# Weaving two instruction streams, a top-k search and four layers, on every engine of one core

## What is computed

```python
xn = _layernorm(x); s = _Ln_attn_ref(xn, ...); g = _silu(_Ln_ffn_ref(xn, ...)); x = x + s * g
```

```python
scores = jnp.einsum('bhnd,bhmd->bhnm', q, k) / jnp.sqrt(D); aw = softmax(scores)
kth = jax.lax.top_k(aw, topk)[0][..., -1:]
aws = aw * (aw >= kth); aws = aws / (aws.sum(-1, keepdims=True) + 1e-08); o_s = aws @ v
o = a * o_s + (1.0 - a) * o_l          # o_l: linear attention over softmax(q), softmax(k)
```

## Time and profile before

| | |
|---|---|
| median of 3 runs | 5734.3 us (5724.26 to 5734.64) |
| the profiled execution, its own time | 5721.85 us |
| its span | 5720.0 us |
| DVE busy, share of the span | 4273.7 us, 75% |
| PE busy | 4228.7 us, 74% |
| ACT busy | 2946.7 us, 52% |
| POOL busy | 2505.1 us, 44% |
| PE's granted clock, mean | 0.896 of full speed |

### The profile page before, as it was taken

The page is one execution under the profiler, slowest core; times in us unless marked ns, Lnnn a source line. Parts: engine busy times, 40 slices in busy tenths (PEclk is TensorE's granted clock), DMA queues, the critical chain, the costliest instruction groups (busy, mean ns, idle before and its releaser), DMA issues. The chain is left out here.

```text
span 5720.0 us, 61822 instructions
## 1 busy us (share of the span) xinstructions
PE 4228.7 (74%) x17108; PEld 2321.5 (41%) x17108; DVE 4273.7 (75%) x8380; ACT 2946.7 (52%) x5759; POOL 2505.1 (44%) x2236
## 2 busy tenths in 40 slices
PE   5876778767787677776777777786777867777676
PEld 2434434334343443434434344342443424434344
DVE  3478964799647995479953899548994489944899
ACT  3544645446454564545645456454554545545455
POOL 0245622446224562245622466214662156621565
PEclk9998989988899898988989978999889998889988
DMA  2000000000000000000000000000000000000000
GB/s 101 1 0 3 1 3 1 0 3 1 3 1 0 3 1 3 1 2 1 1 3 1 2 1 1 3 1 2 1 1 3 1 2 1 1 3 1 2 1 3
DMA packets 3553, 23.17 MB, mean 4 GB/s; under 512 B 336, under 2 KB 336, under 8 KB 2640
## 3 DMA queue, kind: packets, MB, share of 16 engines
q1 hardware_dynamic: 3152, 18.59, 0.8%
HBM read 16.23 MB, written 2.36 MB: 3 GB/s over the span
## 5 line engine op out<-in xcount | busy, mean ns | idle before, releaser
L1662 POOL TENSOR_SCALAR l_pp<-l_sc,l_m 128x512 f32<-128x512 f32 x496 | 781.8, 1576 | 642.6 <-DVE l_m L1612 618.7
L1612 DVE MAX8 l_m<-l_wk 128x8 f32<-128x512 f32 x1536 | 979.9, 679 | 0.0
L1356 PE MATMUL bank<-consts,l_pp 128*128 128x128 f32 x2048 | 396.7, 326 | 499.5 <-POOL l_pp L1669 490.0
L227 PE MATMUL bank<-l_v,l_pt 128*128 128x99 f32 x4096 | 645.6, 311 | 147.4 <-ACT l_pt L1402 131.4
L1432 ACT ACTIVATE l_sc<-bank 128x512 f32<-128x512 f32 x512 | 303.0, 594 | 743.3 <-PE bank L227 742.4
L1608 DVE MATCH_REPLACE8 l_wk<-l_m,l_wk 128x512 f32<-128x512 f32 x1024 | 683.6, 675 | 0.0
L227 PEld LDWEIGHTS bank<-l_v,l_pt 128*128 128x128 f32 x4096 | 610.1, 228 | 177.7 <-ACT l_pt L1402 173.3
L227 PE MATMUL bank<-l_km,hold 128*128 128x512 f32 x1024 | 649.2, 724 | 42.5 <-DVE l_ol L1579 18.1
L1356 PEld LDWEIGHTS bank<-consts,l_pp 128*128 128x128 f32 x2048 | 280.6, 166 | 936.7 <-POOL l_pp L1669 803.8
L1669 POOL TENSOR_TENSOR l_pp<-l_pp,l_ex 128x512 f32<-128x512 f32 x496 | 630.3, 1271 | 26.7 <-ACT l_ex L1439 4.9
L1220 POOL TENSOR_TENSOR l_hc<-l_h,l_cn 128x1024 f32<-128x1024 f32 x128 | 302.4, 2362 | 674.1 <-DVE l_h L1170 674.1
(11 more groups left out here) (359 smaller groups left out, 8347.7 us busy)
## 6 DMA issues: line engine op xcount, KB each, us to landing
weights<-weights_dram SPq DMA_DIRECT2D x1, 11014.0 KB, 28.9
hold<-x_dram SPq DMA_DIRECT2D x9, 256.0 KB, 2.6
out_dram<-x SPq DMA_DIRECT2D x9, 256.0 KB, 3.6
consts<-consts_dram SPq DMA_DIRECT2D x1, 1503.0 KB, 32.0
rotary<-consts_dram SPq DMA_DIRECT2D x1, 1024.0 KB, 34.0
```

The source lines that it names most:

```text
L227: return nc.tensor.matmul(o, lhsT, rhs, start=start, stop=stop)
L1356: r = nc.tensor.transpose(bank[3 + n % 2][:, 128 * k:128 * k + 128], pp[n % 2][:, 128 * k:128 * k + 128], C("ident"))
L1612: nc.vector.max(m8[n % RM][:, k + 1], wk_[n % 2][:]).then_inc(S["top"], 1)
L1662: nc.gpsimd.tensor_scalar(pp[n % 2][:], sc[n % RS][:], m8[n % RM][:, 3, 0:1], None, ALU.is_ge).then_inc(S["kept"], 1)
```

## The change

The search is cut out of layer 3 and becomes a stream of its own, B. Stream A is everything else of an item: layers 0 to 3 with the linear attention, the coupled network and the next item's opening. The new function `run(b, item, search)` issues one block in which each engine's list is A of one item and B of the item before, mixed by `weave`. It is called three times: A of item 0 alone, then a loop of seven with both, then B of item 7 alone. The blocks per item become one; the semaphores are counted on over all layers (class `Marks`) and cleared once per block.

```diff
+ROOM = {"hop": 1.8, "l0": 1.0, "pj": 0.8, "at0": 0.8, "at1": 0.8, "at2": 0.7, "wo": 1.5, "ffn": 1.3,
+        "moe": 1.5, "state": 0.1, "states": 0.1, "busy": 0.3}
+def weave(a, b):
+    room = 0.0
+    for kind in a or ():
+        room += ROOM[kind]
+        while b is not None and room >= 1.0:
+            room -= 1.0
+            next(b, None)
+    for _ in b or ():
+        pass
...
+        run(0, True, False)
+        with nc.Fori(1, B) as b:
+            run(b, True, True)
+        run(B, False, True)
```

A may use only PSUM banks 0 to 3, B has the other four. Therefore:

```diff
-                                mm(bank[n % 2][:], W(f"l1_qkv{i}", lo=128 * n, n=128), hs[:]).then_inc(S["pj"], 1)
+                        if k:
+                            pe.wait_ge(*S("t1", k))
+                        mm(A[0], W(f"l1_qkv{i}", lo=128 * n, n=128), L.hs).then_inc(S["pj"], 1)
...
+                    if n + 1 < NU:
+                        pe.wait_ge(*S("exp", 2 * k + 2))
+                        score(i, n + 1)
+                    turn(i, n, 0)
+                    yield "at0"
+                    turn(i, n, 1)
+                    yield "at1"
```

More of the change, by code:

```diff
@@ L199, in build @@
         banks = ctx.enter_context(nc.psum_tensor("bank", [128, 8, 512], F32))
[L200 removed]
+        A = [banks[:, i] for i in range(4)]
+        X, Y, P = [banks[:, 4], banks[:, 5]], banks[:, 6], banks[:, 7]
         x = sb("x", [128, T])
@@ L1759, in build @@
         with ExitStack() as c0:
-            S = Steps(nc, c0, "first")
-            op = Opening(S, [sb(f"first{i}", [128, T], c0) for i in range(8)], *bank[0:5])
+            own = Marks(nc, c0, "first")
+            S = own.layer(**OPENING, DMA="x0 1")
+            op = Opening(S, Carve(0, ARENA), A[3])
+            now[0] = None
             with nc.Block(no_gpsimd_drain=True) as block:
```

3172 lines of the change are left out of this document (1730 added, 1442 removed).

## The result

The changed kernel takes 5851.95 us (median of 4 runs, 5815.3 to 5862.8) against 5731.24 for the kernel before: ratio 1.020, 95% interval 1.015 to 1.025. It is slower, by 121 us; I had forecast 5320, and 5800 at the most. The profiled execution took 5860.5 us with a span of 5858.7.

A forecast was written before the change was run, and what follows sets the result against it. No engine is full: DVE bounds the search, chains of waits through PE, ACT and DVE bound layers 0 and 1. Fixed 852 us plus 7 periods of 636, with 12 for the median, gives 5320 us; range 5040 to 5800.

The forecast's parts named there:

- DVE's load: DVE's work in one loop period: 531 us before, forecast to fall to 490 us.
- Scans: Layer 2's two scans, 3.36 us before, would take 1.22 us each with decays in PSUM, 15 us less.
- Attention units: Layer 1's 16 units: 5.8 us each from lost banks, 6.2 with the search woven in, 99 us together.
- The hops of the woven period: Chain links in the layers: 2.85 us each in layer 1, set by DVE's work, 20 hops 57 us.
- Table loads: ACT's loads: as many as before (47 for 46), 1.28 us each, listed under priced at nothing.
- The first block's floor: Item 0's layers running alone: layer 0 50 us, layer 3 60, the whole block 485.
- The same layers without the search filled 413 us before: Layers' time per period outside the search; 223 us would then be paid for 279 of search.
- PE's step of the search: PE's time per search step: 0.5 us, from products in groups running beside each other; 0.9 the other end.
- `keep_clock`: Dropping it was priced at nothing; if layer 1's clock fell to 0.86, its projections would take 10 us more.
- Expert transfers: 3 MB sent after the second attention, hidden by some 50 us of other work; uncovered about 10 us per period.
- The rival of contention: DVE and POOL delay each other, PE's groups share nothing: period 665, at worst 693; 5500 to 5722 us; chance 0.16.
- The rival of in-order queues: Search bursts on ACT stall the layers' chains: period up to 726 us, 5934 in all; slower, chance 0.17.

The follow-up runs named there:

- e8_room: Changed kernel with the search's 243 steps spread otherwise: fewer in layers 0 and 2, more in layer 3; 5745 us.
- e11_joined: Changed kernel with steps spread as in e8_room, states' gathering product moved, attention reordered, search's exponentials moved up to three slots; 5713 us.
- e12_joined_more: e11_joined with six more search steps taken from layer 0 (20 left) to layer 1's hops; 5703 us.
- e16_tuned_no_switch: e11_joined with room per slot chosen for fewest table loads and Identity replacing the search's exponential (not a usable kernel); 5707 us.
- e6_attention: Changed kernel with layer 1's attention reordered: a unit's second transposes, their copy and value products come one unit later; 5840 us.
- e5_no_switch: Changed kernel with the search's exponentials replaced by Identity, so the search forces no table load (not a usable kernel); 5644 us.

## Why the prediction was wrong

- **DVE's load**: 490 us forecast (its terms add up to 492), 498 measured. Right, and right that it would not bound the period.
- **Scans** at 1.22: the group L1611 has a mean of 1209 ns against 3.36 us for two in the earlier trace rows. By the lock that the Trainium skill describes for two inputs from SBUF (SBUF — State Buffer, SBUF: two separate sides), the trace agrees: one input now comes from PSUM. The gain went, since the state's chain through PE set 4.3 to 4.5 us and not my 3.9; I had not looked at what stands between C and the next B in PE's list.
- **Attention units**: 5.8 alone and 6.2 woven forecast; 6.3 and 6.5 measured. Half right: I named the serial copies, and left out that the exponentials stand behind both.
- **The hops of the woven period. This is the step that failed.** I took "a hop has slack on ACT, where DVE has 2.85 us of work", so a stretch of hops was to last as long as DVE's work in it and a few us of waits. Layer 0 took 88 us for 70. These are the stretches of layers 1 and 2, in the period shown, that are neither projections, attention, experts nor states:

```profile
1409.50:1423.00 13.50, 9.38 (x32) 3.80 (x32) 11.44 (x25) 8.21 (x17) 6.60 (x8) 0.61 0.09 21
1524.00:1563.00 39.00, 26.10 (x111) 11.56 (x110) 27.86 (x64) 19.84 (x34) 16.73 (x18) 0.87 0.00 0
1666.00:1707.00 41.00, 27.72 (x114) 12.63 (x110) 28.11 (x61) 20.64 (x34) 14.57 (x14) 0.83 0.20 77
1707.00:1732.50 25.50, 18.43 (x81) 9.47 (x82) 24.76 (x58) 16.82 (x28) 11.24 (x14) 0.70 0.00 1
1799.00:1831.00 32.00, 22.14 (x75) 8.97 (x75) 22.82 (x51) 19.84 (x36) 12.12 (x12) 0.61 0.00 0
1903.00:1916.00 13.00, 8.10 (x16) 3.75 (x16) 6.90 (x12) 2.24 (x5) 4.63 (x3) 0.55 0.00 0
```

  Layer 1's are 93.5 us where my terms give 81, layer 2's 70.5 for 56. With layer 0 that is 45 of the 66 us by which layers 0 to 2 were over (projections make 6 or 7, attention 5, states 6, experts 3), and DVE works in 180 us of these 252. Layer 3 came out 6 under. A step of the search costs such a stretch more than its 1.25 us of DVE: layer 0 took 91 us with 31 steps and 78 with 25 (e8_room), and 80 with 25 and 72 with 20 (e11_joined, e12_joined_more; all means of six periods).
- **Table loads**, "as many as before (47 for 46), 1.28 us each", priced at nothing but for 6 us among the experts. The count was right and the conclusion wrong. Not the number but who stands behind one decides: 27 to 32 of the period's 68 us, in layers 0, 1 and 2. This is the part of the failed step that a run shows. The states' product is 7 more, the placing of the steps some 15, and these don't add: with all of them changed and the search's loads gone (e16_tuned_no_switch) the period is 684 us, still 48 over my sum. What makes those 48 stays open.
- **The first block's floor**: layer 0 and layer 3 alone, 50 and 60 us, had no row. The earlier trace rows had layer 0 at 63 already, and nothing in the change shortened its chain; it came out at 64. Layer 3 with the change of blocks, its tail and opening now one hop after another, took 89 for 68. With layer 1 (29) and layer 2 (16) this is the first block's 80 us. It isn't the period's 68: e6_attention shortened the first block by 9 us and the period by nothing, e5_no_switch the period by 27 to 32 and the first block by nothing.
- **"The same layers without the search filled 413 us before"**: so they did, but layer 3's own work ran beside the search and isn't in the 413.
- **PE's step of the search** at 0.5: 201.77 / 224 = 0.90 us alone. The other end of my bounds, at a clock of 0.50. The 16 loads of the earlier trace rows are 64 columns wide and the eight beside them 128, so their equal time was no sign that two groups run beside each other.
- **`keep_clock`** at nothing: right in the loop, and within the noise in the first block.
- **Expert transfers** hidden (no engine waits for a transfer after the setup and the first item's input), last search 308, setup 57 for 53: right, or off by 4 us.
- **The rival of contention**: DVE's instruction with two inputs from SBUF (L798 before, L1182 now) takes 674, 710 and 1695 ns at least, in the middle and at most, for 678, 716 and 1561. Nothing of it shows there; its other half was a PE step of 0.90 us, which came true at a clock of 0.50.
- **The rival of in-order queues**: the right outcome, at 68 us per period over my sum where it had 90, and the right mechanism for the 27 to 32 us that the table loads cost. I gave it 0.17, and what spoke against it, the slack on ACT, was no row but a hope.

## What to carry to other kernels

A weave earns only what is left after the price of making two streams fit together, so cost the layers alone in their new form first, row by row, with their own trace; a stretch that ran at 63 us will not run at 50 because a sum needs it. Ask too what the old order already hid: 57 us of layer 3 ran beside the search here before anything was woven. Then look in each in-order queue for what one stream's rare burst (here two table loads around two exponentials) makes the other wait for: its number of instructions says little, its place much more. And weigh the unwoven first and last blocks: with eight items they were 167 us, more than the weave gained in seven.

The best complete kernel of the study, e12_joined_more, is 0.2 to 0.4% faster than the kernel before and some 2.4% faster than the change.

## What the hardware showed that I had not expected

- The search alone holds PE busy for 67% of its time at a granted clock of 0.50 throughout, the lower level; the kernel before had 70% and 0.86 in the earlier trace rows. With 96 full products more in 305 us, 73% busy, it was 0.92. The form of the products differs too (scores over 32 rows and values into 9 columns in the changed kernel); no run changed the form alone, so which of these matters stays open.
- A table load has no cost beyond its 1.28 us in a busy queue: of the changed kernel's some 360 loads, 300 start within 0.02 us of the end of the instruction before them, and what follows starts, in all but a few, within 0.02 us of theirs. What they cost the program is what waits behind them.
- One program, one execution, two lengths of the same stretch: layer 1 took 297 us in five of the changed kernel's periods and 315 in two, at a clock of 0.87 and 0.78. Its runs spread over 0.8%, those of the kernel before over 0.2%.
